# Score matmuls on half arrays and a new order of the attention slots, in a four-layer transformer kernel in fp32

## The reference

```python
xn = layernorm(x)
s  = attention(xn, Wq, Wk, Wv, Wo)     # 32 heads of 16
g  = silu(ffn(xn))
x  = x + s * g
```

## Time and profile before

| what | us |
|---|---|
| median of three runs | 1434.72 |
| span of the profiled execution, first to last instruction | 1432.5 |
| TensorE busy (matmul) | 1328.4 |
| TensorE weight load busy | 998.8 |
| VectorE busy | 884.6 |
| ScalarE busy | 670.5 |
| GpSimd busy | 389.4 |

### The profile page before, as it was taken

How to read it: one execution, slowest core, us unless ns; L and a number is a source line. 1 busy time by engine, 2 the same in 40 slices (tenths; PEclk the granted TensorE clock), 3 DMA queues, 4 the chain that set the end, 5 groups by cost and what they waited for, 6 DMA issues and landing times.

```text
span 1432.5 us, 22066 instructions
## 1 busy us (share of the span) xinstructions
PE 1328.4 (93%) x8364; PEld 998.8 (70%) x8364; DVE 884.6 (62%) x1661; ACT 670.5 (47%) x1420; POOL 389.4 (27%) x470
## 2 busy tenths in 40 slices
PE   4999899997798999998899999989999879899997
PEld 3888777775465666665688888877777557677775
DVE  7733577777506655567455566467777645777873
ACT  3433365655133654556223333236565447365653
POOL 1000333323011100000433443323343346333331
PEclk9999999999799999999899999999999889999998
DMA  6000000002000000002222232100000300000001
GB/s 261 1 1 0 1 3 2 2 2 97 30 0 1 2 1 2 2 2 92 95 89 88 92 107 89 45 1 2 2 3 2 128 30 1 1 2 2 3 1 60
DMA packets 11610, 48.18 MB, mean 34 GB/s; under 512 B 2793, under 2 KB 3694, under 8 KB 10226
## 3 DMA queue, kind: packets, MB, share of 16 engines
q1 hardware_dynamic: 11506, 46.76, 9.3%
HBM read 44.13 MB, written 2.10 MB: 32 GB/s over the span
## 4 chain that ended last, share of the span: by engine, by line
PE 84%; DVE 10%; ACT 3%; issue 2%; DMA 1%; POOL 0%; SPq 0%; DVEq 0%; ACTq 0%
PE bank L487 18%; PE bank L647 13%; PE bank L518 9%; PE bank L719 7%; PE bank L780 7%; PE bank L685 7%; PE bank L739 7%; PE bank L665 6%; PE bank L691 3%; DVE negmaxs L1370 2%; PE bank L750 2%; DVE negmaxw L1370 2%; PE bank L588 1%; DVE stats L1127 1%; PE bank L760 1%
## 5 line engine op out<-in xcount | busy, mean ns | idle before, releaser
L1572 POOL TENSOR_SCALAR_AFFINE_SELECT probss<-probss 128x512 f32<-128x512 f32 x192 | 134.2, 700 | 334.0 <-ACT probss L1038 334.0
L1370 DVE TENSOR_REDUCE negmaxs<-bank 128x2 f32<-128x512 f32 (+1 forms) x384 | 193.7, 551 | 36.8 <-PE bank L691 35.0
L1038 ACT ACTIVATE probss<-bank 128x256 f32<-128x256 f32 (+1 forms) x384 | 167.9, 492 | 41.9 <-PE bank L719 41.4
L685 PE MATMUL bank<-kTs,qTs 128*128 128x512 f32 (+1 forms) x384 | 135.3, 411 | 5.2 <-DVE kTs L1378 2.8
L1518 POOL TENSOR_TENSOR W_lo<-W_lo_whole,W_hi 128x1536 fp32r<-128x1536 f32 x28 | 98.1, 3504 | 138.4 <-ACT W_hi L889 138.4
L719 PE MATMUL bank<-qTs,kTs 128*128 128x256 f32 (+1 forms) x384 | 117.3, 383 | 4.6 <-ACT probss L1038 3.9
L691 PE MATMUL bank<-mask,identb 128*128 128x256 bf16 x384 | 105.0, 283 | 0.0
L889 ACT ACTIVATE W_hi<-W_lo_whole 128x1536 fp32r<-128x1536 f32 x28 | 41.7, 1488 | 134.7 <-DVE W_lo_whole L1253 134.7
L1378 DVE CAST kTs<-bank 128x512 fp32r<-128x512 f32 x96 | 65.6, 689 | 50.9 <-PE bank L665 50.9
L1274 DVE TENSOR_TENSOR h_lo<-h_lo_whole,h_hi 128x512 fp32r<-128x512 f32 x50 | 73.3, 1465 | 34.9 <-ACT h_hi L911 34.9
L1378 DVE CAST kTw<-bank 128x512 fp32r<-128x512 f32 x64 | 40.9, 685 | 82.3 <-PE bank L665 82.3
(11 more groups left out here) (219 smaller groups left out, 3162.2 us busy)
## 6 DMA issues: line engine op xcount, KB each, us to landing
W_lo_whole<-in_w SPq DMA_DIRECT2D x28, 768.0 KB, 4.2
Wqkv_whole<-in_Wqkv SPq DMA_DIRECT2D x3, 1536.0 KB, 10.6
Wo_lo_whole<-in_Wo SPq DMA_DIRECT2D x4, 1024.0 KB, 6.2
Wqkv<-in_Wqkv SPq DMA_DIRECT2D x1, 3072.0 KB, 10.6
Wdown_whole<-in_Wd SPq DMA_DIRECT2D x1, 2816.0 KB, 15.2
x<-in_x SPq DMA_DIRECT2D x4, 512.0 KB, 5.9
out<-x SPq DMA_DIRECT2D x8, 256.0 KB, 2.2
V_lo_whole<-in_V SPq DMA_DIRECT2D x1, 1408.0 KB
```

What stands on the lines that cost most here:

```text
L685: ins = mm(ps[:, 0:2 * nk].rearrange("p (h k) -> p h k", h=2), A[l].qT[u % 2][:, 2 * g + pl, qb * P:(qb + 1) * P], A[l].kT[u % 2][:, slot: ...
L1038: nc.scalar.activation(A[l].probs[gi % 2][:, kb, par:4:2, q0:SEQ], B.tensor(key)[:, 0:2 * nq].rearrange("p (h q) -> p h q", h=2), ACT.Exp, ...
L1370: v.tensor_reduce(A[l].negmax[u % 2][:, qb, 2 * g + pl:2 * g + pl + 9:8], B.tensor(key)[:, 0:2 * nk].rearrange("p (h k) -> p h k", h=2), A ...
L1572: gp.affine_select(out=blk, in_=blk, compare_op=ALU.is_ge, fill=0.0, base=0, pattern=[[0, 4], [1, P]], channel_multiplier=-1).then_inc(cau ...
```

## The change

The score matmuls no longer run over 128 rows with zeros in half of them: each is made of two matmuls over 64 rows (partitions 0 to 63 and 64 to 127), which write different banks. The key stacks shrink to a quarter (layers 0, 2, 3) and a half (layer 1) of their width, with them the transposes and their copies. The causal mask is added by four matmuls of 64 rows. Row scores and column scores of a slot fill two banks at once, and one instruction of VectorE or ScalarE empties both. PSUM is one tensor, and each purpose has a fixed bank. `claim` waits for whoever held any of the banks. The order within a slot changes on TensorE, ScalarE and VectorE, and projections move from g = 0 and g = 3 to g = 1 and g = 3; output projections of one sequence are spread over two slots of an odd unit. Heads are reordered to fit in the weights' layout. The core of the diff:

```diff
 
+
+ROWS = [(4, 2), (0, 2)]
+COLS = [(2, 2), (6, 2)]
+QKV_BANK = 2
+KEYS_BANKS = {True: (7, 1), False: (4, 2)}
+MAX_BANK = {True: 5, False: 0}
+OUT_BANK = (1, 0)
+
+
+def context_bank(u):
+    return 6 if u < UNITS - 1 else 5
+
+
+def values_bank(l, u):
+    return 4 if GQA[l] or u == UNITS - 1 else 7
+
+
+def rows_turned(u, g):
+
+    if u % 2 == 1 or u == 0 or g < 2:
+        return []
+    if u == UNITS - 2:
+        return [(u // 2 - 1, 0), (u // 2 - 1, 1)] if g == 2 else []
+    return [(u // 2 - 1, g - 2)]
+
+
+def rows_projected(u, g):
+
+    if u == UNITS - 2:
+        return [(u // 2 - 1, 0), (u // 2 - 1, 1)] if g == 3 else []
+    return [(u // 2 - 1, g // 2)] if u % 2 == 1 and 1 < u < UNITS - 1 and g % 2 == 0 else []
+
...
+    def claim(self, key, bank, n=1):
+
+        earlier = [self.emptied(k) for k in dict.fromkeys(self.holder[bank:bank + n]) if k is not None]
+        self.where[key] = (bank, self.uses[bank], n)
...
+        self.holder[bank:bank + n] = [key] * n
+        return self.tensor(key), earlier
...
+            def turn_stacks(l, u, half, bank=2, keys=None):
+
+                keys = keys or KEYS_BANKS[GQA[l]]
+                for tau in range(2):
+                    i = 2 * u + tau
...
+                    key = ("qT", l, u, tau, half)
+                    ps = claim(key, bank + tau)
...
+                n = A[l].kn // 2
+                key = ("kT", l, u, half)
+                if GQA[l]:
+                    ps = claim(key, *keys)[:, 0:2 * P].rearrange("p (t q) -> p t q", t=2)
+                else:
+                    ps = claim(key, *keys)
...
+
                 u, g = divmod(gi, GROUPS)
...
+                key = ("S", l, u, g, qb)
+                ps = claim(key, *(banks or ROWS[qb]))
                 for pl in range(2):
...
+                    for par in range(2):
+                        r = slice(64 * par, 64 * par + 64)
+                        ins = mm(ps[:, par, pl * nk:(pl + 1) * nk], A[l].qT[u % 2][r, 2 * g + pl, qb * P:(qb + 1) * P],
...
+                if CAUSAL[l]:
+                    for j in range(2):
+                        for par in range(2):
+                            r = slice(64 * par, 64 * par + 64)
+                            k0 = nk - P + 64 * j
+                            dst = ps[:, par, 0:2 * nk].rearrange("p (h k) -> p h k", h=2)[:, :, k0:k0 + 64]
+                            ins = mm(dst, cut_rows[r, j, :], cut_keys[r, j, :, :], start=False, stop=(j == 1))
+                ins.then_inc(B.fills(key), 1)
...
+                ps = claim(key, MAX_BANK[GQA[l]])
+                pe.wait_ge(*B.emptied(("S", l, u, GROUPS - 1, 1)))
...
+                key = ("ST", l, u, g, kb)
+                ps = claim(key, *COLS[kb])
+                for pairs in ((0, 2),) if GQA[l] else ((0, 1), (1, 2)):
+                    n = pairs[1] - pairs[0]
+                    for par in range(2):
+                        r = slice(64 * par, 64 * par + 64)
...
+                ins.then_inc(B.fills(key), 1)
+
+            def weigh_values(l, gi, slot):
                 u, g = gi // GROUPS, gi % GROUPS
                 key = ("PV", l, gi)
-                ps, again = B.claim(key, misc_bank())
-                pe.wait_ge(*B.before(key))
+                ps = claim(key, values_bank(l, slot // GROUPS))
                 if CAUSAL[l]:
                     pe.wait_ge(*causal_cut.at(l, 2 * (gi + 1)))
                 else:
-                    pe.wait_ge(*B.emptied(("ST", l, u, g, 1, 1)))
+                    pe.wait_ge(*B.emptied(("ST", l, u, g, 1)))
...
+                            project(l, u, tau, 2 * (2 * u + tau))
+                turn_stacks(l, 0, 0, bank=0, keys=(4, 1) if GQA[l] else (4, 2))
+                turn_stacks(l, 0, 1)
+                project(l, 2, 0, QKV_BANK)
                 for gi in range(GROUPS):
                     for qb in range(2):
-                        scores_rows(l, gi, qb)
-                for tau in range(2):
-                    turn_stacks(l, 1, tau, 0)
+                        scores_rows(l, gi, qb, (ROWS[qb], COLS[1 - qb])[gi % 2])
+                project(l, 2, 1, QKV_BANK)
+                turn_stacks(l, 1, 0)
                 turn_max(l, 0)
                 for qb in range(2):
                     scores_rows(l, GROUPS, qb)
...
-                    if g == 0 and u + 2 < UNITS:
-                        project(l, u + 2, 1)
-                    if g == 3 and u + 3 < UNITS:
-                        project(l, u + 3, 0)
-                    if g == 3 and u + 1 < UNITS:
+                    scores_cols(l, u, g, 0)
+                    if ahead:
+                        scores_rows(l, gi + LEAD, 0)
+                        scores_rows(l, gi + LEAD, 1)
+                    scores_cols(l, u, g, 1)
+                    if gi >= 1:
+                        weigh_values(l, gi - 1, gi)
+                    if g == 0 and u + 1 < UNITS:
+                        turn_stacks(l, u + 1, 1)
+                    if g == 2 and u + 2 < UNITS:
+                        turn_stacks(l, u + 2, 0)
+                    if g % 2 == 1 and u + 3 < UNITS:
+                        project(l, u + 3, g // 2, QKV_BANK)
+                    if gi >= 2:
+                        turn_context(l, gi - 2, gi)
+                    for b, tau in rows_turned(u, g):
+                        turn_rows(l, b, tau)
+                    for b, tau in rows_projected(u, g):
+                        project_out(l, b, tau, 1 if u % 2 == 1 else OUT_BANK[tau])
+                    if g == 2 and u + 1 < UNITS:
                         turn_max(l, u + 1)
-                    scores_cols(l, u, g, 0)
-                    if g == 0 and u + 1 < UNITS:
-
-                        turn_stacks(l, u + 1, 0, 1)
-                    if g == 2 and u + 2 < UNITS:
-
-                        turn_stacks(l, u + 2, 0, 0)
-                    if ahead and g != 1:
-                        scores_rows(l, gi + LEAD, 0)
-                    if gi >= 1:
-                        weigh_values(l, gi - 1)
-                    if ahead and g == 1:
-
-                        scores_rows(l, gi + LEAD, 0)
-                    scores_cols(l, u, g, 1)
-                    if g == 0 and u + 1 < UNITS:
-                        turn_stacks(l, u + 1, 1, 1)
-                    if g == 2 and u + 2 < UNITS:
-                        turn_stacks(l, u + 2, 1, 0)
-                    if ahead:
-                        scores_rows(l, gi + LEAD, 1)
-                    if gi >= 2:
-                        turn_context(l, gi - 2)
-                    if u % 2 == 0 and u > 0 and g == 2:
-                        turn_rows(l, u // 2 - 1)
-                    if u % 2 == 0 and u > 0 and g == 3:
-                        project_out(l, u // 2 - 1)
                     if l + 1 < LAYERS and u == UNITS - 1 and g > 0:
 
                         transposes(l + 1, (2 * g - 2, 2 * g - 1), banks=(0, 1))
...
                 for gi in range(GROUPS * UNITS):
                     u, g = divmod(gi, GROUPS)
-                    if g == 0 and u + 2 < UNITS:
-                        take_projection(l, u + 2, 1)
-                    if g == 3 and u + 3 < UNITS:
-                        take_projection(l, u + 3, 0)
                     exponentials(l, u, g, 0)
-                    if g == 0 and u + 1 < UNITS:
-                        take_stacks(l, u + 1, 0, 1)
-                    if g == 2 and u + 2 < UNITS:
-                        take_stacks(l, u + 2, 0, 0)
+                    exponentials(l, u, g, 1)
                     if gi >= 1:
                         take_pv(l, gi - 1)
-                    exponentials(l, u, g, 1)
                     if g == 0 and u + 1 < UNITS:
-                        take_stacks(l, u + 1, 1, 1)
+                        take_stacks(l, u + 1, 1)
                     if g == 2 and u + 2 < UNITS:
-                        take_stacks(l, u + 2, 1, 0)
+                        take_stacks(l, u + 2, 0)
                     if g < 2 and u + 2 < UNITS:
                         stack_high(l, u + 2, g)
-                    if u % 2 == 0 and u > 0 and g == 2:
-                        take_rows(l, u // 2 - 1)
+                    if g % 2 == 1 and u + 3 < UNITS:
+                        take_projection(l, u + 3, g // 2)
+                    for b, tau in rows_turned(u, g):
+                        take_rows(l, b, tau)
...
-                for pl in range(2):
-                    key = ("S", l, u, g, qb, pl)
-                    dve.wait_ge(*B.filled(key))
-
-                    v.tensor_reduce(A[l].negmax[u % 2][:, qb, 2 * g + pl:2 * g + pl + 9:8],
-                                    B.tensor(key)[:, 0:2 * nk].rearrange("p (h k) -> p h k", h=2),
-                                    AX.X, ALU.max, negate=True).then_inc(B.empties(key), 1)
-
-            def take_key_stacks(l, u, tau, half):
-                for name, w in stack_banks(l, half)[1:]:
-                    key = (name, l, u, tau, w)
-                    dve.wait_ge(*B.filled(key))
```

(39 more changed lines are left out.)

411 lines of the change are left out of this document (188 added, 223 removed).

## The result

The changed kernel took 1524.46 us (median of 4 runs, 1518.44 to 1530.05) against 1435.01 for the kernel before (4 runs, 1433.62 to 1436.25): a ratio of 1.0623, 95% interval 1.0595 to 1.0651. It is 6.2% slower; I had said 1.6%, with a range that ended at 1500. The profiled run took 1525.16 us with a span of 1523.4, 90.9 more than the span before.

A forecast was written before the change was run, and what follows sets the result against it. TensorE's issue bounds the kernel before; after the change the ring does. Span 1432.5 + 15 (causal layers) + 3.3 (layer 1) + 5 (clock) = 1455.8 us, with 2.2 to the median 1457, 1.6% slower; range 1400 to 1500.

The forecast's parts named there:

- ring: In causal layers values wait for VectorE's maximum, itself behind TensorE's context transposes; in layer 1 they wait for ScalarE's exponential.
- clock: TensorE's pauses may lower the granted clock: 5 us taken, bounds nothing and 40 us (40 pauses at 1 us each).
- ring, three causal blocks: Layers 0, 2, 3, values of slot 4 to slot 28: 137.5 us instead of 129.3, +8.1 each.
- ring, layer 1's block: Layer 1, values of slot 4 to slot 28, waiting for the second exponential: 176.1 us against 172.3, +3.8.
- all outside the blocks: Outside slots 4 to 28: per causal layer, stacks stop waiting for VectorE's copies (about -2.3 us), unit 7 gains about 0.8.
- TensorE's terms: Score matmuls of a causal slot: 1.33 us instead of 2.19, two 64-row matmuls taken as fast as one.
- Rival B: Much slower: pairs of 64-row matmuls don't overlap, column and row scores cost what they cost now; 1503 us, chance 0.10.
- the embedding: Causal layers, g = 0 and g = 3: VectorE's rotary embedding lies in the ring and adds 1.72 us.
- Rival C: Slower through the clock: 40 pauses at 1 us each, 1492 us, chance 0.15.
- the shorter key copies: VectorE's copies of the keys: counted as nothing, since VectorE is waiting there.
- Rival A: Faster: VectorE and ScalarE keep ahead, TensorE stays the bound; 1294 us in full, 1365 with half; chance 0.22.

The follow-up runs named there:

- the fill: Changed kernel with score matmuls of layers 0, 2 and 3 repeated in units 1 to 6 while TensorE would be idle: 1509.37 us, ratio 1.0521.
- The fills: Changed kernel with score matmuls repeated in idle TensorE time, in layers 0, 2 and 3 (1509.37 us) or in layer 1 (1515.46 us).

## Why the prediction was right in direction and wrong in size

To part ring and clock, take each of the 24 slots at its shortest among the blocks of the changed kernel and of the one with the fill: 138.1 us in a causal layer. For layer 1 the same over the runs that left it as it was or filled it: 187.8. Both are estimates (neighbouring slots can trade time, and a shortest value may flatter); the filled blocks, 143.3 and 191.6, bound them from above. The rows for ring and clock below rest on them.

| term, us | predicted | measured |
|---|---|---|
| ring, three causal blocks | 3 x 8.1 = 24.3 | 3 x 8.8 = 26.4 |
| ring, layer 1's block | 3.8 | 15.5 |
| clock inside the blocks | 5 | 33.0 + 14.5 = 47.5 |
| all outside the blocks | -9.8 | +1.5 |
| sum | 23.3 | 90.9 |

**TensorE's terms** held in their sum. A pair of 64-row matmuls starts 3 to 4 ns apart, and 512 columns a pair take 0.33 us to the next (260.92 to 261.25; 0.34 predicted). The row scores take less than predicted (270.91 to 271.18 and on to 271.60: 0.27 and 0.42 against 0.40 and 0.46), the second column scores more, mostly 0.29 to 0.32 with the values in bank 3, where the values do not wait, against 0.13: about 1.33 us a slot, as predicted. Rival B, no overlap, is out.

**The ring in the causal layers** held within 0.35 us in each slot of units 1 and 3: maximum 0.688 us (0.684), slots of unit 1 at 5.34, 5.39, 4.55 and 6.00 (5.0, 5.5, 4.4, 6.35), of unit 3 at 8.8, 5.4, 8.1 and 6.0 (8.8, 5.5, 8.2, 6.35), 138.1 us for the block where I had 137.5. Bank 3 for the values and the added wait in the kernel before moved the blocks the way the ring demands. So did the embedding's place, but by 2.5 us only: the embedding stands in the ring as predicted, and moving it between the maxima does not take its full price away. With the bounds of the estimate the ring is worth 26 to 42 us for three layers. Some sums of the working are slightly off (0.70 + 0.34 + 0.64 + 0.78 is 2.46 and not 2.43; 2.85 + 0.44 + 1.33 - 0.75 is 3.87 and not 3.8; the last sum gives 1458, not 1457), too little to matter.

**The step that failed first is the clock, "I take 5, since most pauses are shorter than that row's".** One row with a pause of 2.3 us was no ground to let shorter pauses go free. Of the pauses of TensorE of at least 1.5 us between 186 and 1420 us, 20 of 23 had a stretch at 1.2 GHz begin in them or within 1.5 us after, and 15 of the 50 between 1.0 and 1.5 us. The estimated 47.5 us even lie above my upper bound, 40 pauses at 1 us, and that the two are near each other is luck: the four blocks have 14 pauses of at least 1.5 us and 43 between 1.0 and 1.5, and each of the 26 stretches at 1.2 GHz costs 1.8 us by the estimate. Rival C (1492), to which I gave 0.15, is the case that came, with a longer ring in layer 1 on top. The fills show the clock as cause in part: at clock 1.00 with the ring left in place 17.2 us of the causal blocks go, though the repeats cost time themselves, and 10.7 of layer 1's. So 28 of the 47.5 us are measured, each on one profiled execution (against the two other runs that left the causal blocks alone the 17.2 are 15.6 and 20.7); the rest is the estimate.

**The second step is layer 1's ring, 3.8 against 15.5.** I had values wait for the second exponential, and that holds. Missed was what delays that exponential: the keys' copy of 1024 elements, 1.23 us on VectorE, holds banks 4 and 5 against the next first row scores. TensorE's timeline:

```profile
550.85 0.41 PE L776 MATMUL bank<-ident,pvw 128*128 128x128 f32 x2
551.26 0.50 PE L747 MATMUL bank<-qTw,kTw 64*128 64x256 f32 x4
552.53 0.74 PE L715 MATMUL bank<-kTw,qTw 64*128 64x256 f32 x8 [0.77 <-DVE kTw L1380]
553.08 0.43 PE L747 MATMUL bank<-qTw,kTw 64*128 64x256 f32 x4
```

The row scores start 1.27 us after the column scores instead of 0.31, second column scores and second exponential shift with them. I counted "the shorter key copies" as nothing; in layer 1 two copies had become one twice as long, on banks of the ring. How much of the 11.7 us is this was not tried apart. Where it lies can be read from unit 1 at full clock: the two slots with key copies take 6.22 and 6.54 against 5.5 and 5.35 predicted, 1.9 us together, the two projection slots 9.58 each against 9.3, 0.6 together.

**Outside the blocks** I expected 9.8 us less and measured 1.5 more. 144 us there ran at the 1.2 GHz level against 88 before, and the stretches from the values of slot 1 to those of slot 4 are 0.3 to 5.8 us longer. Whether the clock explains all of this was not tried apart.

**Rival A** (faster) had its condition right, that the ring goes, and its size far too high: with every wait for the ring gone, causal blocks stay at 132 to 134.5, where the rival in full has 99. TensorE's own work is not that short, it is busy 115 us of layer 0's block with bank 3, and 34 waits of 0.15 to 1.3 us are left in the 24 slots, 17 us together, most of them for banks that two purposes share.
